# Rotating three pairs of accumulator banks between score tiles and transposed scores in a long self attention

## The reference, cut to what matters

```
cp = leaky_relu(einsum('btd,cd->btc', x, Wc) + bc)
q, k, v = cp[..., :128], cp[..., 128:256], cp[..., 256:]   # 16 heads of 8, 8 and 64
scores = einsum('bqhd,bkhd->bhqk', q, k) / SCALE
attn   = softmax(scores, axis=-1)
out    = einsum('bhqk,bkhd->bqhd', attn, v)
x      = x + x + leaky_relu(out @ Wo.T + bo)
```

## Time and profile before

| | |
|---|---|
| runs (median) | 2134.19 us |
| profiled execution, its own time | 2132.76 us |
| its span | 2131.0 us |
| TensorE busy | 1814.4 us, 85% |
| VectorE busy | 1087.0 us, 51% |
| ScalarE busy | 850.8 us, 40% |
| GpSimd busy | 516.0 us, 24% |
| mean granted TensorE clock | 0.898 of full speed |

### The profile page before, as it was taken

The page is one execution under the profiler, slowest core; times in us unless marked ns, Lnnn a source line. Parts: engine busy times, 40 slices in busy tenths (PEclk is TensorE's granted clock), DMA queues, the critical chain, the costliest instruction groups (busy, mean ns, idle before and its releaser), DMA issues.

```text
span 2131.0 us, 27189 instructions
## 1 busy us (share of the span) xinstructions
PE 1814.4 (85%) x10505; PEld 1033.6 (49%) x10505; DVE 1087.0 (51%) x2162; ACT 850.8 (40%) x1406; POOL 516.0 (24%) x574
## 2 busy tenths in 40 slices
PE   4598898877997988979888988798988978979888
PEld 3354654633354555543445564434554643455546
DVE  5576476553654553346455534562645255636442
ACT  2222222213643453336343533463534425625342
POOL 2476276200350021005300300071003001700120
PEclk7799899987998989989999898899998988989899
DMA  7000000000000000000000000000000000000000
GB/s 199 1 1 0 0 0 0 0 0 0 1 1 0 1 1 1 6 0 1 1 1 1 1 1 6 0 1 1 1 1 1 1 6 0 1 1 1 1 1 6
DMA packets 18260, 13.27 MB, mean 6 GB/s; under 512 B 7643, under 2 KB 14783, under 8 KB 18143
## 3 DMA queue, kind: packets, MB, share of 16 engines
q1 hardware_dynamic: 17951, 11.65, 1.9%
q10 hardware_dynamic: 192, 0.02, 0.0%
HBM read 10.55 MB, written 1.05 MB: 5 GB/s over the span
## 4 chain that ended last, share of the span: by engine, by line
PE 66%; issue 10%; DVE 7%; ACT 6%; POOL 5%; POOLq 5%; DVEq 1%; DMA 0%; SPq 0%; ACTq 0%
PE PSUM L1255 6%; PE PSUM L1432 5%; PE PSUM L1424 5%; PE PSUM L422 4%; PE PSUM L1332 4%; PE PSUM L1303 4%; PE PSUM L378 3%; PE PSUM L1319 2%; POOLq L863 2%; PE PSUM L1397 2%; POOLq L861 2%; POOL OTA L865 2%; POOL OTA L860 2%; PE PSUM L400 2%; PE PSUM L1315 2%
## 5 line engine op out<-in xcount | busy, mean ns | idle before, releaser
L577 DVE TENSOR_REDUCE negmax<-PSUM 128x2 f32<-128x1024 f32 (+3 forms) x256 | 256.5, 1016 | 138.6 <-PE PSUM L384 81.8
L233 POOL TENSOR_TENSOR rstd<-var,neg_half 128x4 f32<-128x4 f32 (+1 forms) x33 | 33.5, 1015 | 973.9 <-DVE var L223 888.5
L559 ACT ACTIVATE PTA<-PSUM 128x1024 f32<-128x1024 f32 (+1 forms) x224 | 214.3, 963 | 107.3 <-PE PSUM L422 106.3
L1255 PE MATMUL PSUM<-PTA,VA 128*64 128x512 f32 x512 | 146.5, 650 | 4.7 <-ACT OTA L538 2.2
L1687 ACT ACTIVATE PTA<-PSUM,V 128x512 f32<-128x512 f32 x128 | 88.0, 687 | 136.1 <-PE PSUM L1424 133.1
L639 POOL TENSOR_TENSOR QXA<-QXA,PTA 128x1024 f32<-128x1024 f32 x56 | 132.7, 2370 | 35.2 <-ACT PTA L559 31.8
L422 PE MATMUL PSUM<-QSTACK,KSTACK 64*128 64x512 f32 (+3 forms) x512 | 116.0, 473 | 22.3 <-ACT PTA L559 9.0
L2019 DVE TENSOR_REDUCE nmax<-PSUM 128x1 f32<-128x589 f32 x128 | 97.7, 766 | 65.0 <-PE PSUM L1309 65.0
L1424 PE MATMUL PSUM<-YT,W 128*128 128x512 f32 x256 | 127.1, 646 | 0.0
L1432 PEld LDWEIGHTS PSUM<-W,PTA 128*128 128x128 f32 x1024 | 118.2, 192 | 10.0 <-issue 9.9
L1432 PE MATMUL PSUM<-W,PTA 128*128 128x128 f32 x1024 | 119.7, 275 | 0.0
(11 more groups left out here) (415 smaller groups left out, 3709.6 us busy)
## 6 DMA issues: line engine op xcount, KB each, us to landing
W<-in_L_ffn_W_dram SPq DMA_DIRECT2D x1, 2048.0 KB
out_dram<-X SPq DMA_DIRECT2D x4, 256.0 KB, 2.3
PTA<-in_L_attn_Wc_dram SPq DMA_DIRECT2D x1, 640.0 KB
PTA<-in_L_attn_Wo_dram SPq DMA_DIRECT2D x1, 512.0 KB
Wkv<-in_L_xattn_Wkv_dram SPq DMA_DIRECT2D x1, 512.0 KB
KMA<-in_L_attn_ttt_proj_dram SPq DMA_DIRECT2D x1, 256.0 KB
QXA<-in_L_ffn_w_up_dram SPq DMA_DIRECT2D x1, 256.0 KB
QXA<-in_L_ffn_w_down_dram SPq DMA_DIRECT2D x1, 256.0 KB
```

Source lines behind the costliest of these rows:

```text
L559: A.activation(probs, PSUM[:, at:at + 2, 0:probs.shape[2]], ACT.Exp).then_inc(m_exp, 1)
L577: last = Vv.tensor_reduce(negmax[:, s % 2, t, :], PSUM[:, k:k + 2, at:at + a.width(t)], AX.X, ALU.max, negate=True)
L1255: last = T.matmul(PSUM[e * VD:(e + 1) * VD, 6, :], V1[:, c, h * VD:(h + 1) * VD], full.probsT(s, c)[:, e, :], start=(c == 0), stop=(c == Q ...
```

## The change

The transposed scores of the long self attention no longer stay in banks 4 and 5. Score tiles from number 7 on and all transposed scores go through the pairs 0/1, 2/3 and 4/5 in turn, in the order in which TensorE makes them: T0 in 2, tile 7 in 4, T1 in 0, tile 8 in 2, T2 in 4, tile 9 in 0, and so on. The waits follow the banks. `scores_T(k)` waits for the maximum of tile k + 5 (after the last tiles for the exponential of k - 3), and `scores(n)` from tile 8 on waits for the exponential of transposed scores n - 8, which is the one just before its neighbour. No matmul, exponential or reduction is added, removed or put elsewhere.

```diff
             def score_bank(self, n):
                 if self.causal:
                     return 0 if n < 5 else 2 * ((2 * n - 8) % 3)
-                return 0 if n < 6 or n % 2 else 2
+                return 0 if n < 7 else 2 * ((2 * n - 12) % 3)
 
             def scoresT_bank(self, k):
-                return 2 * ((2 * k + 1) % 3) if self.causal else 4
+                return 2 * ((2 * k + 1) % 3)
...
                     if i == 0 or n == 6:
                         pe.wait_ge(m_stacked, a.stacks(b, PAIRS if n == 6 else 2 * (s // 2) + 2))
-                    if n:
-                        pe.wait_ge(m_max, a.tiles(b, n if n < 6 else n - 1))
+                    if n >= 8:
+                        pe.wait_ge(m_exp, a.tiles(b, n - 7))
+                    elif n and n < 7:
+                        pe.wait_ge(m_max, a.tiles(b, n))
...
                 if i == 0:
                     pe.wait_ge(m_rows, a.stacks(b, s + 1))
-                if a.causal:
-                    if k == 0:
-                        pe.wait_ge(m_stacked, a.stacks(b, PAIRS))
-                    elif k + 3 < a.units * PAIRS:
-                        pe.wait_ge(m_max, a.tiles(b, k + 4))
-                    else:
-                        pe.wait_ge(m_exp, a.tiles(b, k - 2))
-                elif k >= 1:
-                    pe.wait_ge(m_exp, a.tiles(b, k))
+                before = k + (3 if a.causal else 5)
+                if k == 0:
+                    pe.wait_ge(m_stacked, a.stacks(b, PAIRS))
+                elif before < a.units * PAIRS:
+                    pe.wait_ge(m_max, a.tiles(b, before + 1))
+                else:
+                    pe.wait_ge(m_exp, a.tiles(b, k - 2))
```

## The result

The changed kernel takes 2115.11 us (four runs: 2107.47, 2115.10, 2115.12, 2115.59) against 2134.23 us (the median with a fourth run of the kernel before, 2135.42), ratio 0.9901 with a 95% interval of 0.9878 to 0.9924. It is 19 us faster, where 7.7 us were forecast. The profiled execution took 2115.12 us, its span is 2113.4 us.

The account below looks back on a forecast made before the run. TensorE was taken to set the attention's pace. 1.3 us from moved waits plus 6.4 us from shorter cross-attention stretches at 1.2 GHz made 7.7 us, giving 2126.5 us; the forecast's own range is 2122 to 2131, the whole range 2114 to 2138.

Parts of the forecast that it names:

- the two places named: Per batch, transposed scores 1 at the loop's start (1.60 us wait) and transposed scores 7 in the second pair (0.66 us).
- The size of the local gain: At the attention's end: 0.30 us from the loop's start plus 0.33 us from the second pair, 0.63 us per batch.
- the step that credits the transposed scores with their full time in front of the wait: At the loop's start: transposed scores 1 run in the gap, winning their 0.59 us, of which 0.30 us is kept.
- the first term: Behind the attention, 0.31 us per batch of the shift is left: 1.3 us in all, ends 0.1 and 2.5 us.
- The second term: Cross attention's 1.2 GHz stretch shrinks from 10.1 to 3.3 us: 2.1 us per batch, 6.4 us for three.
- Rival 3: Once one 1.2 GHz stretch gives way, more do, carrying the next batch along: 2115 to 2120 us; chance 0.09.
- Rival 1: Stretches at 1.2 GHz stay and the shift is swallowed: 2132.9 us; chance 0.32 together with the no-effect case.
- Rival 2: In the attention's opening the clock stays at 2.4 GHz: 12 us over three batches, 2122 us; chance 0.09.
- Rival 4: Transposed scores right behind `value` start 0.10 us sooner, their weight load no longer held: 3.2 us, 2129.7 us; chance 0.05.
- rival 5: Next batch's first-layer cross attention: fall comes 3.4 us sooner, lengthening its 1.2 GHz stretch; slower, 2139.7 us; chance 0.12.

Follow-up runs that it names:

- e2: Changed kernel with one more VectorE copy per batch between attention and cross attention: 2134.53 us.
- e6: Changed kernel, but transposed scores 1 of each batch wait for the first exponential as before; only the later waits are moved: 2133.14 us.
- e10: Kernel before, attention unchanged, with five more VectorE copies per batch between attention and cross attention: 2109.02 us.
- e8: Changed kernel with five more matmuls per batch, result not used, behind transposed scores 1 in the attention's opening: 2123.11 us.

## Why the prediction was right and where it was wrong

**What bounds the kernel, and which waits go.** Right. The waits moved from L422 to L380 at the two places named, no reduction became the bound, and tile 8 and tile 14 wait 1.46 and 0.23 us (1.3 and 0.3 forecast). The first `value` starts 0.34 us sooner after the first transposed scores, not 0.6 (3.15 us, before 3.49).

**The size of the local gain.** 0.34 to 0.42 us came in three batches and 0.92 in the third, 0.63 was forecast. What failed is the step that credits the transposed scores with their full time in front of the wait: the tile behind the wait pays 0.72 us for its start where 0.56 was counted, and it starts later after the first transposed scores (2.43 us against 2.34). At the second place it is the same at 2.4 GHz: 0.43 us (573.23 to 573.66) where 0.33 was counted, so 0.23 us were won and not 0.33. The 0.92 us of the third batch were in no term: there the level falls 0.25 us behind the start of the first transposed scores, in the other batches 0.94 us or more. Over four batches the attention won 2.1 us where the first term had 1.3, so the term came out near for reasons of its own.

**The second term, the cross attention's stretch.** Its mechanism was right: a first turn nearer to the fall gives the short stretch, as e2, e6 and e10 show in both directions. So was its size in itself: 2.0 us in a batch, 2.1 forecast. It came in two batches, not in three, because the gain of the second batch changed where the third meets the fall (0.56 us behind it). The margin was small and not seen: 0.33 us behind the fall was enough in the fourth batch, 0.39 in e6 was not.

**The sum, which was too small by more than half.** The step that failed is that the forecast ended at the cross attention: 1.3 + 6.4 has no term for the stretches behind it and holds them to be as before. In the two batches in which the cross attention ends about 2 us sooner, the 13.3 us at 1.2 GHz in the causal attention's opening don't come at all, which is worth 5.5 us in each, and 3.4 us of the stretch at the experts are saved, worth 0.8 us behind the second batch's causal attention and 1.3 behind the fourth's. That is the larger part of 8 us per batch, and some 13 us of the 17.6. Rival 3 had this kind of effect, at 2115 to 2120 us and with a chance of 0.09; the chance was mis-sized. That its time was met is in part luck: it counted 3.4 us in each of four batches, and it was 9 us in each of two. The trace before had the stretch of 13.3 us in full view, as the longest of each batch, and the prediction does not mention it.

**The rivals.** Rival 1 (swallowed, 2132.9 us) is what most runs of e6 do. Rival 2 (the opening's level does not fall) did not happen; e8 shows that it takes more work in that gap, and that its price was not seen. Rival 4 is out: L422 still starts 1.01 us behind `value` (571.49 to 572.50 in the first batch), with its wait met, and the load of its weights starts at 572.50 too, behind the running matmuls and not ahead of them. Of rival 5, a stretch that gets longer, one is there, though not at the place named: in the first layer of the third batch the stretch of 6.8 us behind that place became one of 10.2. It cost 0.8 us, and 1.5 us were won right behind it, where a stretch of 3.4 us is gone.

**How much time a low stretch costs.** The span times (1 - mean clock) x 2 is the time at 1.2 GHz: 2131.0 x 0.102 x 2 = 435 us before, 2113.4 x 0.090 x 2 = 380 us after. 55 us less at 1.2 GHz came with 17.6 us less time (the moved waits among them), 0.32 us for each. For the kernel with the norms filled it is 2069.5 x 0.055 x 2 = 228 us, 207 us less for 61.5 us, 0.30 for each.

## What to carry to other kernels

A wait on the critical path that goes is worth what then stands at the end of the path, here 0.3 of 2.3 us, since the same exponential was waited for one instruction later. In a kernel whose TensorE clock falls and rises many times, a shift of a third of a microsecond can be worth nothing or 19 us, and an added idle time can make it faster; so look at the granted clock by stretches, all of them and not the next one only, before a small gain or loss is put down to the edit, and test it with a small delay. What helped with either attention was to remove falls: idle TensorE time in front of a stage was filled with matmuls whose result is not used, for 58 to 60 us. It is not wholly steady either, since the runs of one of the two lie 18 us apart, and e8 shows that such matmuls can cost more than they give.

## What the runs showed of the hardware

- Adding work or waiting made the kernel faster: one matmul per batch 13 us, 2.4 us of idle time per batch 25 us, 21 matmuls per batch together with the change 60 us.
- After filling, TensorE stayed at 2.4 GHz for 160 us on end through the gaps of the second batch that had brought it to 1.2 GHz before.
- VectorE instructions of 8 values per partition took 1.49 and 2.22 us beside GpSimd's additions of 128 x 1024 values; their median is 0.18 us.
- The cross attention's first turn started 0.29 to 0.36 us behind a fall of the level in ten batches, and the level was back 3.4 us after the fall; it started 0.39 to 0.76 us behind in 25 batches, and the level was back after 10.2 us.
- A pair of matmuls that starts behind a wait takes 0.72 us to the next instruction at 1.2 GHz, behind running matmuls 0.56 us; at 2.4 GHz it is 0.43 and 0.33 us.
